# V in four pieces, block stores by column, block loads in pairs, first modulation behind the rows

## The chip, the core and the metric

The kernel runs on one core of a Trainium2 chip. The metric is the device time of one execution in microseconds (us). A core has five engines, each with its own instruction queue: TensorE (PE, matmuls), VectorE (DVE), ScalarE (ACT), GpSimd (POOL) and SyncE (SP), which here issues nearly all transfers. The transfers themselves run on 16 DMA engines, which all queues share. Engines wait for each other by semaphores alone.

## What is computed

`x` has 8 batches of 512 rows of 512 values. Two layers are applied, each with a residual:

```python
x = x + L0(x, mask, cond, ...)      # attention
x = x + L1(x, cond, ...)            # quaternion rotation
# L0
q, k, v = (x @ Wq.T, x @ Wk.T, x @ Wv.T)        # 16 heads of 32
scores = einsum('bhsd,bhtd->bhst', q, k) * 32 ** -0.5
attn = softmax(where(mask, -inf, scores))
out = einsum('bhst,bhtd->bhsd', attn, v) @ Wo.T
xn = out / sqrt(mean(out * out) + 1e-6) * rms_scale
shift, sc = split(silu(cond) @ Wc.T + bc)
return xn * (1 + sc) + shift
# L1: a product with a fixed 512 x 512 rotation made of cond, q_right and gate
```

## The kernel before

The first third (`projections`) computes q, k and v of all batches and writes them to scratch memory in HBM. The rest (`attention`) goes through 32 units, a unit being 4 heads of one batch (NG = 4 units in a batch). The order of the work is written out by hand: GROUPS lists the groups of tiles, v counts them. Groups 0 to 29 are whole units of 16 tiles (4 heads i by 4 chunks c of 128 rows), and the last two units are split into four half groups. Each engine runs through the same list of tiles with its own offsets: PE computes scores 7 tiles ahead, DVE adds the mask and finds the row minimum, ACT takes the exponential, then a tile of probabilities must be transposed before it can be multiplied by V.

Three of the four heads of a unit are transposed on PE (L831) and copied out of PSUM by ACT (L1074) or DVE (L965). The first head (i = 0) goes another way. DVE transposes its four tiles in blocks of 32 x 32 (`block`, L956) into `blocks`, with partitions (a, p), a = 0 to 3, p = 0 to 31, and free dimensions (k, j, c, t). What is left, to exchange blocks a and k, is done by two transfers through the scratch `blocks_scratch`, of 1 MB each way: four stores (L749), one for each a, from 32 partitions, and four loads (L755), one for each a, into `turned_probs`. Each load waits for its own store (`blocks_out[a]`, L754). DVE may overwrite `blocks` for the next group when all four stores have landed (L951). PE multiplies a group by V (`values`, L866) two tiles into the next group; its first head waits for the loads (`moved`).

SP's queue is in order. For each group v it does, in this order: the result store of an earlier chunk and the load of an x chunk (both wait for GpSimd); `move_blocks(v)`, the stores and loads above; `load_unit(u + 2)`, eight loads of 256 KB with the rows of q and k for the unit after the next; at the first group of a batch the modulation (`load_mod`, 512 KB, one row of 4 KB to all partitions); and at the second group of a batch the whole V of the next batch (`load_v`, 1 MB). In group 4 (v == NG) V of batch 1 and the modulation of batch 0 are loaded first, ahead of the group's block stores. GpSimd needs the modulation in `shift` (L1177), the last thing in its list for group 4; in its list for group 5 stand `rms` (L1183) and `spread_inverse` (L1155), whose result PE transposes in `turn_scale` (L840).

Two buffers each of V and the modulation alternate by batch. The semaphore `v_in[b % 2]` tells PE that V of batch b is there.

Of the kernel before, what the change touches and what calls it, by code (L numbers as in the profile page):

```python
# [14 lines left out]
B, S, E = 8, 512, 512  # L15
H, D = 16, 32
C = 128
KC = E // P
TC = S // P
HG = P // D  # L20
NG = H // HG
# [3 lines left out]
RING, SLOTS = 10, HG + 1  # L25
# [59 lines left out]
def f32(ap):  # L85

    return ap.bitcast(F32)
# [514 lines left out]
def attention(nc, held, block, banks, x, scr, rows, scores, late, late_x, kept, done, mod_scr, out, rot, ident, wo_hi,  # L602
# [5 lines left out]
    with ExitStack() as ctx:  # L608
        def sb(name, shape, dt=F32):
            return ctx.enter_context(nc.sbuf_tensor(name, shape, dt))  # L610

        def sem(name):
            return held.enter_context(nc.semaphore(name))
# [7 lines left out]
        v_sb = f32(values_and_k[:, :, :, :])  # L621
        turned_probs = sb("turned_probs", [P, SLOTS, TC, S])
        blocks = sb("blocks", [P, TC, TC, TC, D])
# [20 lines left out]
        v_in = kept.v_in  # L644
# [3 lines left out]
        out_act, out_dve = sem("out_act"), sem("out_dve")  # L648
        scale_turned, scale_out = sem("scale_turned"), sem("scale_out")
        valued, normed = sem("valued"), sem("normed")  # L650
        blocks_out = [sem(f"blocks_out{a}") for a in range(TC)]
        moved = sem("moved")
        o_hi_ready, o_ready = sem("o_hi_ready"), sem("o_ready")
        y_ready = sem("y_ready")
        squared = sem("squared")
# [22 lines left out]
        def outs(eng, n):  # L678

            return BY_ACT[:n + 1].count("1" if eng == "act" else "0")  # L680
# [16 lines left out]
        def span(chunks):  # L697

            return slice(chunks[0] * P, (chunks[-1] + 1) * P)
# [34 lines left out]
        @block.sync  # L734
        def _(sp):
            def load_unit(u):
                if u >= 2:
                    sp.wait_ge(scored, TILES * (u - 1))
                for r in range(4):
                    rows.load_q(sp, u, r)  # L740
                    if u < U - 1:
                        rows.load_k(sp, u, r)

            def move_blocks(v):
                sp.wait_ge(blocked, TC * (v + 1))
                if v >= 2:
                    sp.wait_ge(moved, 16 * TC * (v - 1))
                for a in (0, 2, 1, 3):
                    sp.dma_start(scr["blocks"][v % 2, a].rearrange("(k p) t -> p k t", p=D),  # L749
                                 blocks[a * D:(a + 1) * D].rearrange("p k j c t -> p k (j c t)")).then_inc(blocks_out[a], 16)  # L750
                if v >= 2:
                    sp.wait_ge(valued, v - 1)
                for a in (0, 2, 1, 3):
                    sp.wait_ge(blocks_out[a], 16 * (v + 1))  # L754
                    sp.dma_start(turned_probs[:, HG * v % SLOTS, a, :], scr["blocks"][v % 2, a]).then_inc(moved, 16)  # L755

            def load_v(b):
                if b >= 2:
                    sp.wait_ge(valued, NG * (b - 1))
                if b == B - 1:  # L760
                    sp.wait_ge(held_stored, 16 * TC)
                sp.dma_start(v_sb[:, b % 2], scr["v"][b].rearrange("c p e -> p c e")).then_inc(v_in[b % 2], 16)

            def load_mod(b):
                if b >= 2:
                    sp.wait_ge(summed, TC * (b - 1))
                sp.dma_start(mod[:, b % 2], mod_scr[b].partition_broadcast(P)).then_inc(mod_in[b % 2], 16)

            def load_x(b, c):
                if TC * b + c >= 2:  # L770
                    sp.wait_ge(rotated, TC * b + c - 1)
                sp.dma_start(x_s[:, c % 2], x[b, c * P:(c + 1) * P, :]).then_inc(x_in[c % 2], 16)

            def store(m):
                b, c = m // TC, m % TC
                sp.wait_ge(rotated, m + 1)
                sp.dma_start(out[b, c * P:(c + 1) * P, :], acc[:, c % 2]).then_inc(stored[c % 2], 16)

            def store_held(c):
                sp.wait_ge(held_copied, c + 1)  # L780
                sp.dma_start(scr["v"][B - 1, c], held_v).then_inc(held_stored, 16)

            for j in range(4):
                sp.wait_ge(qk_stored[j], 16 * 4 * B)
            sp.wait_ge(mod_stored, 16)
            for v, (u, chunks) in enumerate(GROUPS):
                b, g = u // NG, u % NG
                if v == NG:
                    sp.wait_ge(held_made, TC)
                    load_v(1)  # L790
                    load_mod(0)
                if 1 <= v <= NG:
                    store_held(v - 1)
                if NG <= v < NG + LATE_X:
                    load_x(v // NG - 1, v % NG)
                if v >= NG + 2:
                    store(v - NG - 2)
                if chunks == ALL:
                    move_blocks(v)
                if u + 2 < U:  # L800
                    load_unit(u + 2)
                if v == V - 6:
                    sp.wait_ge(valued, NG * (B - 1))
                    for r in range(4):
                        rows.load_k(sp, U - 1, r)
                if g == 0 and b > 0:
                    load_mod(b)
                if g == 1 and 0 < b < B - 1:
                    load_v(b + 1)
                if v == V - 5:  # L810
                    for c in range(TC):
                        sp.dma_start(late_x[:, c], x[B - 1, c * P:(c + 1) * P, :]).then_inc(late_in[c], 16)
            store(CHUNKS - 1)
            for j, m in enumerate(LATE):
                sp.wait_ge(late_rotated, j + 1)
                sp.dma_start(out[m // TC, m % TC * P:(m % TC + 1) * P, :], late_out[j]).then_inc(late_stored[j], 16)
            for j in range(2):
                sp.wait_ge(stored[j], 16 * len(range(j, CHUNKS, 2)))
            for j in range(3):
                sp.wait_ge(late_stored[j], 16)  # L820

        @block.tensor
        def _(pe):
# [20 lines left out]
            def values(v, part):  # L844

                u, chunks = GROUPS[v]
                b, g, cols = u // NG, u % NG, span(chunks)
                if part == 0 and v % NG == 0:
                    pe.wait_ge(v_in[b % 2], 16 * (b // 2 + 1))
                if part == 0:  # L850
                    if v == 0:
                        pe.wait_ge(qk_lo_ready, 2 * NG * B)
                    pe.wait_ge(out_act, outs("act", FIRST[v + 1] - 1))
                    pe.wait_ge(out_dve, outs("dve", FIRST[v + 1] - 1))
                    if v > 0:
                        pe.wait_ge(normed if v <= POOL_GROUPS else o_ready, v)
                for i in range(HG):
                    h = HG * g + i
                    to, of = value_ps[i * D:(i + 1) * D, cols], turned_probs[:, (HG * u + i) % SLOTS, part, cols]
                    if i == 0 and chunks == ALL:  # L860
                        if part == 0:
                            pe.wait_ge(moved, 16 * TC * (v + 1))
                        to = to.rearrange("p (c a t) -> p a c t", c=TC, a=TC)
                        of = turned_probs[:, HG * u % SLOTS, :, part * P:(part + 1) * P].rearrange(
                            "p a (c t) -> p a c t", c=TC)
                    last = pe.matmul(to, v_sb[:, b % 2, part, h * D:(h + 1) * D], of,  # L866
                                     start=(part == 0), stop=(part == TC - 1))
                if part == TC - 1:
                    last.then_inc(valued, 1)
# [35 lines left out]
            for n, (v, u, i, c) in enumerate(ORDER):  # L905
                t = n - FIRST[v]
# [19 lines left out]
            for part in range(TC):  # L926
                values(V - 1, part)
# [13 lines left out]
        def _(dve):  # L941
# [7 lines left out]
            def block(n):  # L949
                v, u, i, c = ORDER[n]  # L950
                dve.wait_ge(exped, n + 1)  # L951
                if n == 0:
                    dve.wait_ge(projected, (TC + 2 * NG) * (B - 1) + 2 * NG)
                for a in range(TC) if c == 0 and v > 0 else ():
                    dve.wait_ge(blocks_out[a], 16 * v)
                dve.transpose(blocks[:, :, :, c, :].rearrange("p k j t -> p j k t"),  # L956
                              probs[:, n % RING, :].rearrange("p (j k t) -> p j k t", j=TC, k=TC)).then_inc(blocked, 1)

# [68 lines left out]
            for n, (v, u, i, c) in enumerate(ORDER):  # L1027
                t = n - FIRST[v]
# [282 lines left out]
```

## Time and profile before

| | us |
|---|---|
| median of 3 runs (lowest to highest) | 828.29 (827.21 to 829.35) |
| the profiled execution | 826.24 |
| its span, from the first to the last instruction | 824.4 |
| PE busy, share of the span | 799.9, 97% |
| ACT busy | 605.8, 73% |
| DVE busy | 606.6, 74% |
| GpSimd busy | 517.5, 63% |
| DMA: moved, mean rate | 216.63 MB, 263 GB/s |

The attention part begins at about 260 us, where the page's slices of DVE and ACT fill up. Busy time of PE is modelled and includes overlapping instructions. A number in brackets behind a row of the timeline is the idle time of the engine ahead of it, and what ended it.

### The profile page before, as it was taken

What the parts mean: (1) busy time and instruction counts of PE and PEld (TensorE: products, weight loads), DVE (VectorE), ACT (ScalarE), POOL (GpSimd) and SP (SyncE); (2) the same over time, 40 slices, a digit from 0 to 9 for tenths busy, and PEclk for the clock granted to TensorE, in tenths of its full rate; (3) what the DMA queues carried; (4) which work ended last, traced back from release to release, by engine and by line L of the source; (5) the groups of instructions that cost most, each with busy time, mean ns of one, the idle gap of its engine ahead of it and who ended that gap; (6) DMA issues with size and microseconds to landing.
All of it is one profiled execution on the core that took longest, in us unless ns stands there. A gap on an engine that the chain in (4) does not pass through costs nothing.

```text
span 824.4 us, 16423 instructions
## 1 busy us (share of the span) xinstructions
PE 799.9 (97%) x4864; PEld 597.2 (72%) x4864; DVE 606.6 (74%) x1495; ACT 605.8 (73%) x1504; POOL 517.5 (63%) x375
## 2 busy tenths in 40 slices
PE   9999999999998999999999999998999999999887
PEld 6788888888887776677677767775677677767664
DVE  4612313213227899999999999999899999997666
ACT  6222222323326899999999999999999999998772
POOL 0899992000000111288888887888788888888984
PEclk9999999999999899999999999999999999999999
DMA  8964555546388888999998999898989998998001
GB/s 286 339 222 179 204 188 207 191 155 227 128 307 290 288 279 287 331 336 322 324 319 307 305 322 334 291 307 293 321 304 336 328 313 295 327 319 294 27 27 52
DMA packets 116912, 216.63 MB, mean 263 GB/s; under 512 B 12360, under 2 KB 13000, under 8 KB 116832
## 3 DMA queue, kind: packets, MB, share of 16 engines
q1 hardware_dynamic: 116688, 215.42, 76.4%
q8 instruction: 36, 0.59, 0.3%
q14 instruction: 44, 0.36, 0.1%
q10 hardware_dynamic: 144, 0.26, 0.1%
HBM read 133.81 MB, written 81.82 MB: 262 GB/s over the span
## 4 chain that ended last, share of the span: by engine, by line
ACT 21%; PE 16%; POOL 10%; issue 8%; DMA 7%; DVE 3%; SPq 3%; DVEq 0%; ACTq 0%; POOLq 0%
ACT probs L156 15%; PE banks L831 5%; DMA blocks_scratch<-blocks 5%; ACT turned_probs L1074 5%; PE banks L866 4%; POOL late L711 4%; PE banks L137 4%; DMA turned_probs<-blocks_scratch 3%; POOL late L1212 2%; SPq L749 1%; PE banks L900 1%; PE banks L880 1%; ACT o_T L1106 1%; DVE blocks L956 1%; ACT inv_T L1090 1%
## 5 line engine op out<-in xcount | busy, mean ns | idle before, releaser
L156 ACT ACTIVATE probs<-probs,least 128x512 f32<-128x512 f32 x512 | 376.3, 775 | 3.1 <-DVE least L148 3.1
L148 DVE CUSTOM_DVE_ANT_0 probs<-banks,mask_bias 128x512 f32<-128x512 f32 x512 | 327.7, 681 | 11.3 <-PE banks L137 9.9
L831 PE MATMUL banks<-ident,probs 128*128 128x128 f32 x1568 | 232.0, 274 | 0.0
L831 PEld LDWEIGHTS banks<-ident,probs 128*128 128x128 f32 x1568 | 191.9, 141 | 43.2 <-issue 6.7
L137 PE MATMUL banks<-k_rows,q_rows 128*128 128x512 f32 x496 | 201.4, 456 | 5.8 <-DVE least L148 5.8
L1074 ACT ACTIVATE turned_probs<-banks 128x512 f32<-128x512 f32 x256 | 159.6, 643 | 16.9 <-PE banks L831 11.9
L419 DVE SCALAR_TENSOR_TENSOR late<-banks,late 128x512 fp32r<-128x512 f32 x64 | 44.0, 690 | 160.0 <-ACT late L356 160.0
L156 ACT ACTIVATION_READ_ACCUMULATOR probs<-probs,least 128x1 f32 x512 | 129.8, 254 | 0.0
L711 POOL TENSOR_TENSOR late<-rot,late 128x2048 f32<-128x2048 f32 x28 | 128.9, 4604 | 0.0
L356 ACT ACTIVATE late<-banks 128x512 fp32r<-128x512 f32 x64 | 38.2, 598 | 119.3 <-PE banks L492 113.7
L866 PE MATMUL banks<-turned_probs,v_sb 128*32 128x512 f32 (+1 forms) x1088 | 116.9, 570 | 9.1 <-DMA turned_probs<-blocks_scratch 7.6
L137 PEld LDWEIGHTS banks<-k_rows,q_rows 128*128 128x128 f32 x496 | 90.7, 190 | 35.8 <-issue 24.3
L965 DVE COPY turned_probs<-banks 128x512 f32<-128x512 f32 x136 | 93.3, 686 | 1.8 <-PE banks L831 1.6
L866 PEld LDWEIGHTS banks<-turned_probs,v_sb 128*32 128x32 f32 x1088 | 34.1, 109 | 72.2 <-issue 59.9
L1217 POOL MEMSET minus_half<- 128x1 f32 x1 | 0.1, 98 | 132.8 <-PE banks L831 132.8
L956 DVE STREAM_TRANSPOSE blocks<-probs 128x512 f32<-128x512 f32 x120 | 75.0, 680 | 0.0
L1212 POOL TENSOR_TENSOR late<-late 128x1024 f32<-128x1024 f32 x29 | 69.4, 2393 | 2.2
L349 ACT ACTIVATE v_out<-banks 128x512 f32<-128x512 f32 x28 | 16.7, 598 | 56.3 <-PE banks L492 53.0
L1164 POOL CAST o_hi<-o_T 128x512 fp32r<-128x512 f32 x29 | 17.8, 613 | 63.8 <-DVE o_T L977 56.5
L900 PE MATMUL banks<-wo_hi,o_hi 128*128 128x512 f32 x128 | 50.8, 397 | 2.4 <-DVE late L1002 2.4
L900 PE MATMUL banks<-wo_lo,o_hi 128*128 128x512 f32 x128 | 52.8, 413 | 0.0
L900 PE MATMUL banks<-wo_hi,o_lo 128*128 128x512 f32 x128 | 50.5, 395 | 0.0
(136 smaller groups left out, 1331.9 us busy)
## 6 DMA issues: line engine op xcount, KB each, us to landing
q_rows<-q_scratch SPq DMA_DIRECT2D x128, 256.0 KB, 4.7
k_rows<-k_scratch SPq DMA_DIRECT2D x124, 256.0 KB, 4.9
blocks_scratch<-blocks SPq DMA_DIRECT2D x120, 256.0 KB, 5.2
turned_probs<-blocks_scratch SPq DMA_DIRECT2D x120, 256.0 KB, 3.4
q_scratch<-late SPq DMA_DIRECT2D x64, 256.0 KB, 2.3
k_scratch<-late SPq DMA_DIRECT2D x64, 256.0 KB, 2.3
v_sb<-v_scratch SPq DMA_DIRECT2D x8, 1024.0 KB, 7.8
out<-late SPq DMA_DIRECT2D x29, 256.0 KB, 5.7
```

Of the source, the lines that this page charges most:

```text
L137: pe.matmul(self.ps[:, n % SCORE_BANKS, :], self.rows.q[:, u % 2, i, c * P:(c + 1) * P], self.rows.k_of(u)[:, i, :], start=True, stop=True ...
L148: dve.tensor_tensor_reduce(self.probs[:, n % RING, :], self.ps[:, n % SCORE_BANKS, :], self.mask_bias[:, c, :], 1.0, 3e38, ALU.add, ALU.mi ...
L156: act.activation(self.probs[:, n % RING, :], self.probs[:, n % RING, :], ACT.Exp, bias=self.least[:, n % 32:n % 32 + 1], scale=-1.0, accum ...
L419: dve.scalar_tensor_tensor(qk_lo[m % 4], proj[:, m % 4, :], QSCALE if m < NG else 1.0, late[:, m % 4, :], ALU.mult, ALU.subtract).then_inc ...
L711: return eng.tensor_tensor(to.rearrange("p j (i d) -> p j i d", i=4), rot[:, :, :, :], chunk.rearrange("p (j d) -> p j d", j=4).unsqueeze( ...
L831: last = pe.transpose(turn_bank("tile", n)[:, j * P:(j + 1) * P], probs[:, n % RING, j * P:(j + 1) * P], ident[:, :])
L866: last = pe.matmul(to, v_sb[:, b % 2, part, h * D:(h + 1) * D], of, start=(part == 0), stop=(part == TC - 1))
L900: last = pe.matmul(y_of(m), left[:, b % 2, k, t], right[:, k, :], start=(part == 0), stop=(part == 11))
L956: dve.transpose(blocks[:, :, :, c, :].rearrange("p k j t -> p j k t"), probs[:, n % RING, :].rearrange("p (j k t) -> p j k t", j=TC, k=TC) ...
L965: dve.tensor_copy(turned_probs[:, h % SLOTS, :, c * P:(c + 1) * P], turn_bank("tile", n).rearrange("p (j t) -> p j t", j=TC)).then_inc(out ...
L1074: act.activation(turned_probs[:, h % SLOTS, :, c * P:(c + 1) * P], turn_bank("tile", n).rearrange("p (j t) -> p j t", j=TC), ACT.Copy).the ...
L1212: pool.tensor_tensor(mix[:, 0:2, :], mix[:, 0:2, :], mix[:, 2:4, :], ALU.add).then_inc(paired, 1)
```

## The change

Stores: the four transfers of a group now go by k, the second of the free dimensions of `blocks`, each from all 128 partitions (a, p); on the scratch side one writes for each a the 32 rows of block column k. `blocks_out` counts by k. Loads: two transfers, each for two values of a, issued when all four stores have landed; `moved` becomes two semaphores, by parity of the group. V: `load_v` takes the chunks to load. Batch 1 is still loaded at once in group 4; V of a later batch comes in four pieces, behind the row loads of the second, third and fourth group of the batch before, and ahead of the block stores of its own first group. The first modulation is loaded in group 4 behind the row loads.

```diff
--- before.py
+++ after.py
@@ -648,8 +648,8 @@
         out_act, out_dve = sem("out_act"), sem("out_dve")
         scale_turned, scale_out = sem("scale_turned"), sem("scale_out")
         valued, normed = sem("valued"), sem("normed")
-        blocks_out = [sem(f"blocks_out{a}") for a in range(TC)]
-        moved = sem("moved")
+        blocks_out = [sem(f"blocks_out{k}") for k in range(TC)]
+        moved = [sem(f"moved{i}") for i in range(2)]
         o_hi_ready, o_ready = sem("o_hi_ready"), sem("o_ready")
         y_ready = sem("y_ready")
         squared = sem("squared")
@@ -744,22 +744,25 @@
             def move_blocks(v):
                 sp.wait_ge(blocked, TC * (v + 1))
                 if v >= 2:
-                    sp.wait_ge(moved, 16 * TC * (v - 1))
-                for a in (0, 2, 1, 3):
-                    sp.dma_start(scr["blocks"][v % 2, a].rearrange("(k p) t -> p k t", p=D),
-                                 blocks[a * D:(a + 1) * D].rearrange("p k j c t -> p k (j c t)")).then_inc(blocks_out[a], 16)
+                    sp.wait_ge(moved[v % 2], 32 * (v // 2))
+                to = scr["blocks"][v % 2].rearrange("a (k p) t -> a p k t", p=D)
+                for k in range(TC):
+                    sp.dma_start(to[:, :, k], blocks[:, k].rearrange("p j c t -> p (j c t)")).then_inc(blocks_out[k], 16)
                 if v >= 2:
                     sp.wait_ge(valued, v - 1)
-                for a in (0, 2, 1, 3):
-                    sp.wait_ge(blocks_out[a], 16 * (v + 1))
-                    sp.dma_start(turned_probs[:, HG * v % SLOTS, a, :], scr["blocks"][v % 2, a]).then_inc(moved, 16)
-
-            def load_v(b):
+                for k in range(TC):
+                    sp.wait_ge(blocks_out[k], 16 * (v + 1))
+                for a in range(0, TC, 2):
+                    sp.dma_start(turned_probs[:, HG * v % SLOTS, a:a + 2, :],
+                                 scr["blocks"][v % 2, a:a + 2].rearrange("a p t -> p a t")).then_inc(moved[v % 2], 16)
+
+            def load_v(b, chunks):
                 if b >= 2:
                     sp.wait_ge(valued, NG * (b - 1))
                 if b == B - 1:
                     sp.wait_ge(held_stored, 16 * TC)
-                sp.dma_start(v_sb[:, b % 2], scr["v"][b].rearrange("c p e -> p c e")).then_inc(v_in[b % 2], 16)
+                sp.dma_start(v_sb[:, b % 2, chunks], scr["v"][b, chunks].rearrange("c p e -> p c e")).then_inc(
+                    v_in[b % 2], 16)
 
             def load_mod(b):
                 if b >= 2:
@@ -787,14 +790,15 @@
                 b, g = u // NG, u % NG
                 if v == NG:
                     sp.wait_ge(held_made, TC)
-                    load_v(1)
-                    load_mod(0)
+                    load_v(1, slice(0, TC))
                 if 1 <= v <= NG:
                     store_held(v - 1)
                 if NG <= v < NG + LATE_X:
                     load_x(v // NG - 1, v % NG)
                 if v >= NG + 2:
                     store(v - NG - 2)
+                if g == 0 and b >= 2:
+                    load_v(b, slice(TC - 1, TC))
                 if chunks == ALL:
                     move_blocks(v)
                 if u + 2 < U:
@@ -803,10 +807,12 @@
                     sp.wait_ge(valued, NG * (B - 1))
                     for r in range(4):
                         rows.load_k(sp, U - 1, r)
+                if v == NG:
+                    load_mod(0)
                 if g == 0 and b > 0:
                     load_mod(b)
-                if g == 1 and 0 < b < B - 1:
-                    load_v(b + 1)
+                if g > 0 and 0 < b < B - 1:
+                    load_v(b + 1, slice(g - 1, g))
                 if v == V - 5:
                     for c in range(TC):
                         sp.dma_start(late_x[:, c], x[B - 1, c * P:(c + 1) * P, :]).then_inc(late_in[c], 16)
@@ -846,7 +852,7 @@
                 u, chunks = GROUPS[v]
                 b, g, cols = u // NG, u % NG, span(chunks)
                 if part == 0 and v % NG == 0:
-                    pe.wait_ge(v_in[b % 2], 16 * (b // 2 + 1))
+                    pe.wait_ge(v_in[b % 2], 16 + 64 * (b // 2))
                 if part == 0:
                     if v == 0:
                         pe.wait_ge(qk_lo_ready, 2 * NG * B)
@@ -859,7 +865,7 @@
                     to, of = value_ps[i * D:(i + 1) * D, cols], turned_probs[:, (HG * u + i) % SLOTS, part, cols]
                     if i == 0 and chunks == ALL:
                         if part == 0:
-                            pe.wait_ge(moved, 16 * TC * (v + 1))
+                            pe.wait_ge(moved[v % 2], 32 * (v // 2 + 1))
                         to = to.rearrange("p (c a t) -> p a c t", c=TC, a=TC)
                         of = turned_probs[:, HG * u % SLOTS, :, part * P:(part + 1) * P].rearrange(
                             "p a (c t) -> p a c t", c=TC)
@@ -951,8 +957,8 @@
                 dve.wait_ge(exped, n + 1)
                 if n == 0:
                     dve.wait_ge(projected, (TC + 2 * NG) * (B - 1) + 2 * NG)
-                for a in range(TC) if c == 0 and v > 0 else ():
-                    dve.wait_ge(blocks_out[a], 16 * v)
+                for k in range(TC) if c == 0 and v > 0 else ():
+                    dve.wait_ge(blocks_out[k], 16 * v)
                 dve.transpose(blocks[:, :, :, c, :].rearrange("p k j t -> p j k t"),
                               probs[:, n % RING, :].rearrange("p (j k t) -> p j k t", j=TC, k=TC)).then_inc(blocked, 1)
```

## Rows read from the trace of the kernel before

**Rows 1.** The page: span, PE's busy time, DMA share by slice (tenths).

```profile
span 824.4 us, 16423 instructions
...
PE 799.9 (97%) x4864; PEld 597.2 (72%) x4864; DVE 606.6 (74%) x1495; ACT 605.8 (73%) x1504; POOL 517.5 (63%) x375
...
DMA  8964555546388888999998999898989998998001
```

**Rows 2.** Waits: engine, line, releaser, us in total, times, longest.

```profile
PE banks L866 <- DMA turned_probs<-blocks_scratch: 7.6, 6, 2.9
...
SPq L754 <- DMA blocks_scratch<-blocks: 64.9, 26, 5.3
```

**Rows 3.** Timeline of PE, four value groups: start, us, instruction, idle before.

```profile
458.21 2.35 PE L866 MATMUL banks<-turned_probs,v_sb 128*32 128x512 f32 x20
...
507.61 3.64 PE L866 MATMUL banks<-turned_probs,v_sb 128*32 128x512 f32 x32 [0.94 <-DMA turned_probs<-blocks_scratch]
...
575.03 3.64 PE L866 MATMUL banks<-turned_probs,v_sb 128*32 128x512 f32 x32 [2.92 <-DMA turned_probs<-blocks_scratch]
...
754.25 3.64 PE L866 MATMUL banks<-turned_probs,v_sb 128*32 128x512 f32 x32 [1.10 <-DMA turned_probs<-blocks_scratch]
```

**Rows 4.** Timeline of SP's queue: a plain group, then one after V.

```profile
445.60 2.58 SPq L749 DMA_DIRECT2D blocks_scratch<-blocks  x4
450.49 3.16 SPq L755 DMA_DIRECT2D turned_probs<-blocks_scratch  x4
...
494.40 2.07 SPq L749 DMA_DIRECT2D blocks_scratch<-blocks  x4
501.57 2.14 SPq L755 DMA_DIRECT2D turned_probs<-blocks_scratch  x4
```

**Rows 5.** The page's DMA issues: count, KB each, median us from issue to landing.

```profile
blocks_scratch<-blocks SPq DMA_DIRECT2D x120, 256.0 KB, 5.2
turned_probs<-blocks_scratch SPq DMA_DIRECT2D x120, 256.0 KB, 3.4
...
out<-late SPq DMA_DIRECT2D x29, 256.0 KB, 5.7
...
mod_b<-mod_scratch SPq DMA_DIRECT2D x8, 512.0 KB, 7.0
```

**Rows 6.** DMA of 229.9:230.35 (the modulation's store ends), then 798.3:801.5 (one store).

```profile
DMA packets 9, 0.00 MB, mean 9 GB/s; under 512 B 8, under 2 KB 8, under 8 KB 9
...
DMA packets 144, 0.26 MB, mean 82 GB/s; under 512 B 16, under 2 KB 16, under 8 KB 144
...
out<-late SPq DMA_DIRECT2D x1, 256.0 KB, 2.0
```

**Rows 7.** Stretches: length, busy us of each engine, clock, DMA share, GB/s.

```profile
279.13:344.88 65.75, 64.37 (x449) 45.81 (x449) 65.19 (x179) 65.35 (x171) 12.22 (x16) 1.00 0.90 294
344.88:754.25 409.37, 402.76 (x2798) 287.96 (x2799) 398.25 (x1069) 404.91 (x1074) 346.73 (x246) 1.00 0.94 316
```

**Rows 8.** DMA of 344.88:754.25, then of 20:33 with its rates by slice.

```profile
DMA packets 69534, 129.52 MB, mean 316 GB/s; under 512 B 7462, under 2 KB 7462, under 8 KB 69479
...
GB/s 397 378 233 334 271 372 397 391 391 391 384 410 366 365 384 372 384 391 397 410 403 403 410 403 403 403 403 403 410 410 416 403 410 391 403 416 397 410 410 410
DMA packets 2572, 5.05 MB, mean 388 GB/s; under 512 B 166, under 2 KB 166, under 8 KB 2571
```

**Rows 9.** Timeline of SP and PE: first group's stores, loads and values.

```profile
266.49 2.63 SPq L749 DMA_DIRECT2D blocks_scratch<-blocks  x4
271.85 2.25 SPq L755 DMA_DIRECT2D turned_probs<-blocks_scratch  x4
...
279.13 3.64 PE L866 MATMUL banks<-turned_probs,v_sb 128*32 128x512 f32 x32
```

**Rows 10.** Timeline of GpSimd and PE: inverses of group 4.

```profile
343.80 0.61 POOL L1155 COPY inv_d<-inv 128x512 f32<-128x512 f32 x1
...
349.22 0.60 PE L840 MATMUL banks<-ident,inv_d 128*128 128x128 f32 x4
```

## The prediction

> **What bounds the kernel now.** I read the page's busy shares and slices first [rows 1], then the waits of TensorE and of SP's queue [rows 2], then the value matmuls one group at a time [rows 3] and SP's queue around two groups [rows 4]. The reader should see two things. The attention part is filled on every side: in the 409.37 us from the values of group 4 to those of group 29, PE, ACT and DVE are busy 402.76, 404.91 and 398.25 us, and the DMA engines 0.94 of the time at 316 GB/s [rows 7]. That is 25 groups of 16.4 us. And the one thing from outside the compute engines that stops PE is the load of the transposed block: 7.6 us in 6 waits [rows 2], 2.92 us the longest; a group without it starts its values with no wait [rows 3]. Five of the six follow the 1 MB V load or, at the first, V and mod together; the last (1.10 us) follows the loads of K. In the group after a V load the first block comes back 7.2 us after the first store was issued (494.40 to 501.57), in a plain group 4.9 us (445.60 to 450.49) [rows 4]. So the margin is thin in both directions: little to win, about 7 us, and everything that makes stores or loads longer by more than a microsecond or two is paid in every group.
>
> **The edits, one by one.**
>
> *V in four pieces, mod behind the rows.* The bytes stay. Three more issues a batch on SP, about 0.5 us each as the block transfers are (2.14 us for four [rows 4]), against two fewer issues in each group: nothing on the path. The gain is bounded by the waits behind V: 7.6 less the 1.10 of the K loads, 6.5 us [rows 2, 3]. The price is the first modulation: its load goes from before the stores of group 4 to after that group's eight row loads. GpSimd's first shift waits for it, and queued behind that shift stand the first rms and the spread of group 4's inverses, which ran at 343.80 and which PE transposed at 349.22 [rows 10]. The load takes 7.0 us [rows 5], so one wait of 0 to 6 us appears there, once; I take 5 where nothing else is late and nothing where PE is late by more anyway.
>
> *Two loads for four.* A load used to be issued as its own store landed; now both wait until all four have landed. The data are the same 1 MB. Between the first and the last of four issues lay 2.14 and 3.16 us [rows 4], and the last took 3.4 us to land [rows 5], which in the plain group gives 453.65 + 3.4 = 457.1 against values at 458.21 [rows 3]: 1.1 us of cover. Bounds: from 1 us gained (fewer transfers) to 1 us lost in each group.
>
> *Stores by column.* This decides. Before, a store had 32 partitions outermost on both sides. Now the SBUF side has 128 partitions, but the scratch side is written as (a, p, t): 4 outermost, then 32 rows, then 2 KB, and those two cannot be merged, since column k takes 32 rows out of each block of 128. What does a small outermost count do? The trace has one transfer that can be seen alone: the store of the modulation from 8 partitions. Its end holds 8 packets under 512 B (the ninth is a row of data), where one store of 128 partitions ends with 16 among its 144 [rows 6]; those small ones are the completions of the engines that took part. So 8 outermost rows ran on 8 of the 16 DMA engines. No row shows 4 against 128. The two ends are 16 engines, where the store costs what it did, and 4, where each engine carries a quarter of every store. I take 4, since the 8-row transfer is the nearest row.
>
> The Trainium skill has a rule for the case that no row shows ("DMA: Bandwidth & Descriptors", section "Why a DMA increments its semaphore by 16 and not by 1"): a transfer uses the largest number of engines up to 16 that divides the outermost counts of both sides, and on SP's queue they are the lowest-numbered. The trace agrees at 8; by that rule all four stores of a group share the same four engines and the time is the forecast below, and by 16 engines it is one of the rivals at 820 to 835.
>
> Now the price on four engines. The stage moves 129.52 MB in 25 groups [rows 8], 5.18 MB each. Four block stores of 0.26 MB [rows 6] are 1.05 MB of it. Each of the four engines then carries 1.05/4 = 0.262 MB of stores and (5.18 - 1.05)/16 = 0.258 MB of the rest, 0.520 MB, where it carried 0.324 MB. Its rate: 316 GB/s at a share of 0.94 is 21.0 GB/s for a busy engine [rows 7]; in the fullest early stretch 388 GB/s are 24.3 GB/s [rows 8]. The stores meet little else, so 0.262 at 24.3 gives 10.8 us; the rest at the middle of the two rates, 22.6, gives 11.4 us. These follow one another: SP issues the stores, waits for all of them, then issues the loads, then rows, V, x and out, and the next stores stand behind those. Between the last store and the first load the four engines are empty: a store alone takes 2.0 us from issue to landing for about 0.7 us of data [rows 6], so about 1.3 us of start and end, with the issue 1.5 us. **One group: 10.8 + 11.4 + 1.5 = 23.7 us** in place of 16.4. PE, ACT and DVE keep their 16 us and wait for the rest; DVE's next transposes wait for the stores to land, but then take their turn while SP is still issuing rows, so they add nothing. That wait stands in DVE's queue ahead of the masks, and hence of PE's scores: it ends before PE's own wait for the load does.
>
> **Sum.** 25 groups of 23.7 us are 592.5 in place of 409.4: +183. The four groups before (65.75 us at 294 GB/s [rows 7], 4.83 MB each) have 0.236 MB of the rest, 10.4 us, so 22.7 each: +25. The first group, 266.49 to 279.13 [rows 9], had its first store back after 5.4 us and now has it after some 12, less the cover before 279.13: +4. The late mod and V pieces lie inside these waits: 0. The half groups at the end move no blocks: 0. Together +212 on the profiled execution's 826.24, 1038; the median of the runs, 828.29, lies 2 above that execution, so **1040 us**. Low end: 25.6 GB/s, the 410 GB/s of the best slices in the early stretch, and half the gap: 21.0 and 20.2 us, +131, 959. High end: 21.0 GB/s throughout and a gap of 1.8: 26.6 and 25.5 us, with 6 at the start +298, 1126.
>
> **Rivals.** *Faster:* the stores spread over all 16 engines. Then the V pieces take the five waits away and the mod load lands while PE has other work: 826.2 - 6.5, about 820 us. For it: the five waits do follow V. Against: the scratch pattern, and [rows 6]. It decides if the stores show 16 completions each, and the block is back before 7 us have gone.
> The Trainium skill speaks for this rival ("SBUF — State Buffer", section "Door 1: The DMA port swizzle"): 32 adjacent partitions reach half of SBUF's DMA ports, 128 reach all. By that rule the old stores are held at half rate and the new ones come back sooner, 820 us; the trace doesn't bear it out, since the 32-partition stores land in 5.2 us beside 5.7 us for the 128-partition out stores [rows 5].
>
> *A little slower:* 16 engines, or four different ones for each store, but the loads start only after the last store, and mod is late. Half of the 1 us lost in some 20 groups is +10, mod +5, V -6.5: 835 us. For it: the cover of 1.1 us; against, again, the small outermost count.
>
> *No change:* 16 engines, and the gains and the late starts cancel: 826 to 829 us.
>
> **Chances.** Four shared engines, the forecast: 0.86. Faster at 820: 0.04. Slower at 835: 0.07. No change: 0.03. A measurement of this kernel tells about 0.3% from no change. So faster 0.04, same 0.03, slower 0.93. The forecast's bounds, 959 to 1126, hold most of its 0.86, about 0.8 in all, so they are the range.
>
> **What would show it.** Right: groups of 21 to 27 us from one value matmul to the next; PE's wait for the block about 7 us in each of some 29 groups; the first wait of SP for a store over 10 us; landings of the block stores at 10 us and more; a DMA share in the stage of about two thirds or less, because twelve engines idle while four are full; completion packets of 4 a store, some 1,440 fewer in the whole run. Wrong: stores that land in 5 us, or a share that stays above 0.9. If stores are slow but groups stay under 20 us, the step that adds the rest of the traffic behind the stores is the false one; if groups are near 27 us, the rate.

## The result, and the profile after

The changed kernel takes 1058.92 us (median of 4 runs, 1057.90 to 1061.42), 1.279 times the kernel before (827.75 us beside it; interval 1.275 to 1.283). It is slower, and by nearly what was forecast (1040 us). First the page of after: busy times, DMA share by slice, and the counts of DMA packets; the last row is the count on the page of before.

```profile
span 1057.3 us, 16416 instructions
...
PE 858.1 (81%) x4864; PEld 610.9 (58%) x4864; DVE 610.5 (58%) x1495; ACT 610.6 (58%) x1504; POOL 517.3 (49%) x375
...
DMA  9755554558555655556666555655666665556401
...
DMA packets 114800, 216.62 MB, mean 205 GB/s; under 512 B 10248, under 2 KB 10888, under 8 KB 114720
...
DMA packets 116912, 216.63 MB, mean 263 GB/s; under 512 B 12360, under 2 KB 13000, under 8 KB 116832
```

The bytes are the same and DVE, ACT and GpSimd are busy as long as before (PE's busy time is longer; the last section says why); what fell is the DMA share in the attention part, from nines to fives and sixes [rows 1]. Fewer small packets are left, 10248 of 12360. If each of 120 stores ends with 4 completions in place of 16 (-1440), 60 loads are gone (-960) and 18 pieces of V have come (+288), 10248 should remain, and 10248 there are. So the counts fit four engines for every store by column.

The stretches of after that answer to [rows 7]: the four groups before group 4 and the 25 groups behind it (length, busy us of each engine, clock, DMA share, GB/s).

```profile
287.32:381.88 94.56, 71.89 (x448) 47.71 (x449) 63.72 (x171) 64.28 (x166) 9.50 (x11) 0.86 0.57 203
381.88:986.78 604.90, 450.48 (x2798) 298.42 (x2799) 400.51 (x1069) 408.93 (x1070) 351.95 (x254) 0.86 0.60 215
```

The span grew by 232.9 us: 195.5 in the 25 groups (604.90 against 409.37), 28.8 in the four before (94.56 against 65.75), 8.2 in the start of the first values (287.32 against 279.13), 0.4 at the end. A group takes 24.2 us. PE's waits for the block, and one group on SP's queue and on PE:

```profile
PE banks L872 <- DMA turned_probs<-blocks_scratch: 180.8, 30, 10.4
```

```profile
457.49 5.02 SPq L750 DMA_DIRECT2D blocks_scratch<-blocks  x4
473.44 0.90 SPq L756 DMA_DIRECT2D turned_probs<-blocks_scratch  x2
...
481.51 0.58 SPq L750 DMA_DIRECT2D blocks_scratch<-blocks  x1
```

```profile
454.18 5.23 PE L872 MATMUL banks<-turned_probs,v_sb 128*32 128x512 f32 x32 [5.99 <-DMA turned_probs<-blocks_scratch]
```

PE waited for the block in 6 groups before [rows 2], and now waits in all 30, 180.8 us in all. From the first store to the first load there are 15.95 us (457.49 to 473.44), where [rows 4] have 4.9 to 7.2.

Which engines the stores share can be read from the DMA share of that group, in three stretches (their bounds were read off in steps of 0.4 us):

```profile
462.20:472.60 10.40, 9.71 (x63) 7.97 (x62) 10.22 (x32) 10.40 (x28) 9.63 (x5) 1.00 0.26 101
472.60:475.00 2.40, 0.00 (x0) 0.00 (x0) 2.20 (x7) 2.40 (x7) 2.23 (x4) 0.89 0.12 21
475.00:486.40 11.40, 7.81 (x51) 3.88 (x52) 3.81 (x9) 3.65 (x11) 2.09 (x3) 0.72 1.02 358
```

In the first stretch the four stores are issued (the last at 462.51) and little else is left, and about a quarter of the 16 engines is busy, at 101 GB/s, 25 for each of four. So the four stores of a group share the same four engines; had each had four of its own, all 16 would have been busy. In the second the engines are nearly empty, until the first load's data move; in the third the rest of the traffic fills all 16.

### The profile page after: what moved, and what is told of

Same layout as the page of the kernel before. It is cut to its first block, busy times and chain, and to the rows that moved or that the text cites. A ratio compares the mean times of both kernels' runs of the same rounds, so it can differ in the third digit from the quotient of the medians.

```text
span 1057.3 us, 16416 instructions
## 1 busy us (share of the span) xinstructions
PE 858.1 (81%) x4864; PEld 610.9 (58%) x4864; DVE 610.5 (58%) x1495; ACT 610.6 (58%) x1504; POOL 517.3 (49%) x375
## 2 busy tenths in 40 slices
DMA packets 114800, 216.62 MB, mean 205 GB/s; under 512 B 10248, under 2 KB 10888, under 8 KB 114720
## 4 chain that ended last, share of the span: by engine, by line
DMA 35%; PE 32%; SPq 22%; issue 6%; POOL 4%; DVE 1%; ACT 0%; DVEq 0%; POOLq 0%; ACTq 0%
DMA blocks_scratch<-blocks 32%; PE banks L490 8%; PE banks L492 8%; PE banks L491 8%; SPq L107 6%; SPq L103 6%; SPq L750 5%; PE banks L872 2%; PE banks L837 2%; SPq L756 2%; PE banks L137 2%; DMA turned_probs<-blocks_scratch 2%; POOL late L711 1%; SPq L764 1%; PE banks L906 1%
## 5 line engine op out<-in xcount | busy, mean ns | idle before, releaser
L156 ACT ACTIVATE probs<-probs,least 128x512 f32<-128x512 f32 x512 | 364.0, 723 | 2.2 <-DVE least L148 2.2
L872 PE MATMUL banks<-turned_probs,v_sb 128*32 128x512 f32 (+1 forms) x1088 | 171.3, 789 | 181.9 <-DMA turned_probs<-blocks_scratch 180.8
L1080 ACT ACTIVATE turned_probs<-banks 128x512 f32<-128x512 f32 x256 | 149.3, 596 | 230.1 <-PE banks L872 216.9
L872 PEld LDWEIGHTS banks<-turned_probs,v_sb 128*32 128x32 f32 x1088 | 45.7, 145 | 287.9 <-issue 282.9
L156 ACT ACTIVATION_READ_ACCUMULATOR probs<-probs,least 128x1 f32 x512 | 102.7, 201 | 0.0
L1183 POOL TENSOR_TENSOR late<-late,mod_b 128x512 f32<-128x512 f32 x28 | 35.7, 1275 | 35.2 <-DMA mod_b<-mod_scratch 24.0
```

Of the source, the lines that this page charges most:

```text
L156: act.activation(self.probs[:, n % RING, :], self.probs[:, n % RING, :], ACT.Exp, bias=self.least[:, n % 32:n % 32 + 1], scale=-1.0, accum ...
L1080: act.activation(turned_probs[:, h % SLOTS, :, c * P:(c + 1) * P], turn_bank("tile", n).rearrange("p (j t) -> p j t", j=TC), ACT.Copy).the ...
```

## The experiments

Three questions were open: whether the stores alone make the time, whether it is the count of engines or the pattern of the rows, and what the other edits do by themselves.

**Undo the stores alone.** The changed kernel, stores per block a from 32 partitions as before.

```diff
-    for k in range(TC): sp.dma_start(to[:, :, k], blocks[:, k] ...)
+    for a in (0, 2, 1, 3): sp.dma_start(scr["blocks"][v % 2, a] ..., blocks[a * D:(a + 1) * D] ...)
```

> The changed kernel with its four stores put back to one per block a, from 32 partitions each; V in pieces, the late modulation and the two loads stay. My theory (four shared DMA engines carry every store by column): the stores run on 16 engines again and groups fall from 24.2 to 16.2 to 17 us; 815 to 840 us. Rival (the loads that wait for all four stores, the pieces of V or the late modulation make the time): stays above 1000 us. Completion packets: the 120 stores end with 16 each again, so under 512 B 10248 + 1440 = 11688.

Measured: 848.79 us, 1.024 times before (1.017 to 1.031); under 512 B 11688 packets, as worked out. 210 of the 231 us go with the stores. The remaining 21 us lie above the range expected, so the other edits cost something too: PE waits for the block 17 times, and once, 5.7 us, for the inverses.

```profile
PE banks L872 <- DMA turned_probs<-blocks_scratch: 21.3, 17, 4.5
```

**The stores alone.** The kernel before, stores by column, four loads that wait for all stores, since each now needs all of them.

```diff
-    for a in (0, 2, 1, 3): sp.dma_start(scr["blocks"][v % 2, a] ..., blocks[a * D:(a + 1) * D] ...)
+    for k in range(TC): sp.dma_start(to[:, :, k], blocks[:, k] ...)
+    for k in range(TC): sp.wait_ge(blocks_out[k], 16 * (v + 1))
```

> The kernel before with the stores by column alone; still four loads, but each waits for all four stores, since each now needs all of them; V whole and the first modulation early as before. My theory: nearly the whole loss, 1045 to 1075 us, groups of about 24 us. Rival (the other edits): 815 to 850 us. The whole 1 MB of V ahead of the stores may make the groups after it some us longer than others, but the four engines carry the same bytes.

Measured: 1077.93 us, 1.302 times (1.293 to 1.312), a little above the range and 19 us slower than the whole change. Its PE waits 201.7 us for the block, in 30 waits. The stores alone explain the loss. Beside them the other edits give 19 us back, while they lose 21 us without them. The trace shows two places for it. SP needs some 1.75 us to issue the four loads of a group, where two take some 0.9 in after; and a group that starts right behind a whole V is longer (511.75 to 537.82, 26.1 us; the next one 23.4 us). No run separates the two.

```profile
529.61 1.76 SPq L756 DMA_DIRECT2D turned_probs<-blocks_scratch  x4
```

**Two engines.** The changed kernel, each store cut into two of 64 partitions: 2 outermost on the scratch side, the same rows to the same places.

```diff
-    sp.dma_start(to[:, :, k], blocks[:, k] ...)
+    for a in (0, 2):
+        sp.dma_start(to[a:a + 2, :, k], blocks[a * D:(a + 2) * D, k] ...)
```

> The changed kernel with each store by column cut into two of 64 partitions, so that the scratch side is 2 outermost in place of 4; the same rows of 2 KB to the same places, 8 transfers a group in place of 4. My theory, by the same sum: two shared engines carry 1.05/2 = 0.52 MB of stores at 24.3 GB/s, 21.6 us, + 11.4 + 1.5 = 34.5 us a group, 10.8 us more than on four engines in some 29 groups: about 1370 us (1300 to 1450), and 2 completion packets a store. Rival (the scattered rows in scratch, or reading all 128 partitions, make a store slow, whatever the count of engines): the same rows, so near 1059 us, up to 1100 for four more issues.

Measured: 1353.97 us (one run), inside the range. The 25 groups from the values of group 4 to those of group 29, then 12 us in which little but stores is left:

```profile
427.37:1281.64 854.27, 457.64 (x2798) 299.73 (x2799) 402.10 (x1069) 408.90 (x1070) 351.81 (x254) 0.75 0.43 152
...
510.00:522.00 12.00, 4.53 (x28) 3.45 (x27) 5.92 (x19) 8.55 (x24) 8.07 (x7) 0.80 0.13 51
```

A group takes 34.2 us (854.27 / 25) against 34.5 worked out. While the stores run alone the DMA share is 0.13 at 51 GB/s: two engines of 16, at 25 GB/s each, as in after. There are again 10248 packets under 512 B, 2 for each of 240 half stores. The rows and the bytes are those of after, and the half transfers are even smaller, so neither the scattered rows nor the reading of many partitions makes the time; the outermost count does. From four engines to two a group grew by 10.0 us (34.2 against 24.2), where the sum has 10.8.

**All partitions on 16 engines.** The scratch is laid out by column, so that a store has 128 outermost on both sides. The loads go by k into 32 partitions, each behind its own store.

```diff
-    to = scr["blocks"][v % 2].rearrange("a (k p) t -> a p k t", p=D)
-    sp.dma_start(to[:, :, k], blocks[:, k] ...)
+    sp.dma_start(scr["blocks"][v % 2, k], blocks[:, k] ...)
...
-    for a in range(0, TC, 2):
-        sp.dma_start(turned_probs[:, HG * v % SLOTS, a:a + 2, :], ...)
+    for k in range(TC):
+        sp.wait_ge(blocks_out[k], 16 * (v + 1))
+        sp.dma_start(turned_probs[k * D:(k + 1) * D, HG * v % SLOTS], scr["blocks"][v % 2, k].rearrange("(a p) t -> p a t", p=D))
```

> The changed kernel with the scratch laid out by column: a store by column goes from all 128 partitions to 128 rows of 2 KB in a row, so that 128 is outermost on both sides; the loads then go by k into 32 partitions each, and each waits for its own store alone. V in pieces and the late modulation stay. My theory: 16 engines, groups of 16.1 to 16.6 us, 812 to 835 us, 16 completions a store. Rival (reading a column from all 128 partitions is what is slow): above 900 us.

Measured: 830.30 us, 1.002 times (0.999 to 1.005): the same as before, inside the range. Stores land in 4.1 us (5.2 before [rows 5], 4.7 with V in pieces alone), and PE waits for the block 3 times in place of 6. What keeps it from being faster is one place, on PE's timeline:

```profile
346.27 3.64 PE L871 MATMUL banks<-turned_probs,v_sb 128*32 128x512 f32 x32
356.75 1.11 PE L845 MATMUL banks<-ident,inv_d 128*128 128x128 f32 x4 [5.97 <-POOL inv_d L1160]
371.11 1.48 PE L871 MATMUL banks<-turned_probs,v_sb 128*32 128x512 f32 x9
```

From 346.27 to 371.11 there are 24.8 us where a group takes 16.2: PE stands for the inverses of group 4, and those stand on GpSimd behind the shift that waits for the late modulation.

**The other edits, one by one, and a better pair.** Each was made alone in the kernel before (V in pieces with the `load_v` lines of the change); the last row of the table is the run with the scratch by column, its modulation back ahead of the stores.

```diff
# mod alone
-    if v == NG: load_v(1); load_mod(0)
+    if v == NG: load_v(1)          # and load_mod(0) behind load_unit
# pairs alone
-    for a in (0, 2, 1, 3): wait blocks_out[a]; load block a
+    for a in (0, 2, 1, 3): wait blocks_out[a]
+    for a in (0, 2): load blocks a, a + 1
# pairs, each behind its own two stores
+    for a in (0, 1): wait blocks_out[a], blocks_out[a + 2]; load blocks a, a + 2
```

> The kernel before with the first modulation alone moved behind the row loads of group 4. My theory: PE's transposes of the inverses of group 4 wait for GpSimd, which waits for the modulation; the scratch-by-column run shows 8.7 us there (371.11 - 346.27 against 16.1). Here the stores of group 4 are also freed of 0.5 MB, worth at most the 1.4 us that its values waited. So +4 to +9 us, 832 to 837. Rival (hidden, and group 4 gains): 826 to 828 us.

> The kernel before with the two loads alone, which wait for all four stores (from 32 partitions, as before). My theory: the loads come back up to 1 to 2 us later, where the cover is about 1 us; small waits in more than the six groups, 834 to 846 us. Rival (fewer transfers gain as much): 825 to 830 us.

> The kernel before with V alone in four pieces. My theory of the waits behind V: four of the six waits (0.4, 0.9, 2.9, 0.9 us) go and the first stays, 820 to 825 us. Rival (the pieces only spread the same delay over more groups): 826 to 830 us.

> The scratch-by-column run with the first modulation put back ahead of the stores of group 4; V in pieces. My theory: the 8.7 us of that run's group 5 go, about 1.4 us in group 4 come back: 819 to 825 us, faster than the kernel before by 0.4 to 1%. Rival (the wait there has another cause): 828 to 832 us.

> The kernel before with two loads in place of four, each waiting for its own two stores alone (blocks 0 and 2, then 1 and 3, in the order of the stores), beside the run with two loads that wait for all four (847 us). My theory (the wait for all four is what costs): most of those 20 us go, 826 to 836 us. Rival (a load of 512 KB is itself slower to land than two of 256 KB): stays at 840 to 850 us.

| run | us | ratio (interval) |
|---|---|---|
| mod alone | 833.47 | 1.008 (1.005 to 1.011) |
| pairs alone, behind all four stores | 847.23 | 1.024 (1.019 to 1.029) |
| pairs, behind their own two | 840.26 | 1.012 (1.004 to 1.019) |
| V in pieces alone | 825.21 | 0.998 (0.994 to 1.001) |
| scratch by column, V in pieces | 822.29 | 0.994 (0.991 to 0.997) |

The late modulation costs 6 us, V in pieces gains 2 to 3, which the interval can't tell from nothing. The pairs cost 20 us, 1 us more than the range expected. Waiting for their own two stores they still cost 12 (3 to 16 by the interval): above my range and at the low end of the rival's. So the wait for all four has a part, some 8 us (each run against the kernel before beside it); what is left belongs to the larger load, which lands in 4.4 to 4.5 us where one of 256 KB takes 3.4 [rows 5], and to the wait for the second of its stores, and no run separates those two. In both runs PE waits 20 us or more for the block, in 9 and 10 places. V in pieces came out between my range and the rival's; the other two runs lie inside mine.

The last run is the one that beats the kernel before, by 0.3 to 0.9%. In its stage DMA is busy 0.99 of the time and a group takes 16.2 us (405.69 / 25), what PE, ACT and DVE need:

```profile
345.54:751.23 405.69, 403.00 (x2798) 287.70 (x2799) 398.48 (x1069) 404.86 (x1076) 347.28 (x246) 1.00 0.99 319
```

## Why the prediction was right

- *Stores on four engines.* Right, and shown four ways: by the count of completion packets, by the DMA share while the stores run alone (0.26), by the run that undoes the stores, and by the run on two engines. The signs named for it came: groups of 24.2 us, a DMA share of 0.60, and in each of 30 groups a wait for the block, of 6.0 us on average.
- *The price of a group.* 23.7 us worked out, 24.2 measured. In the three stretches above the stores take 10.4 us (10.8 in the sum) and the rest 11.4 (11.4); between the last store and the data of the first load lie 2.4 us where the sum has 1.5. So the gap is the term that was too small; the two groups behind that one divide nearly alike.
- *The sum.* Short by 21 us of 233: +195.5 for +183 in the 25 groups, +28.8 for +25 in the first four, +8.2 for +4 at the start, 0.4 at the end.
- *The other edits at nothing.* Not so, and here luck helped: the stores alone take 250 us more than the kernel before, where the sum gave the whole change 212. The 19 us that the other edits give back beside them brought the measured time nearer to 1040.
- *The start.* The prediction had the first store back some 12 us behind its issue; the first load was issued 14.5 us behind the first store (267.60), which is 2.5 us of the missing 4. The stores themselves were issued 1.1 us later than before [rows 9].

```profile
282.15 0.90 SPq L756 DMA_DIRECT2D turned_probs<-blocks_scratch  x2
```

- *DVE's wait for the stores costs nothing.* Right: its transposes begin at 473.50, 0.06 us behind the first load's issue, and are done long before SP's next stores at 481.51.

```profile
473.50 2.49 DVE L962 STREAM_TRANSPOSE blocks<-probs 128x512 f32<-128x512 f32 x4 [0.20 <-DMA blocks_scratch<-blocks]
```

- *The late modulation, hidden where PE is late anyway.* The wait came, 4.46 us at the inverses of group 4, and the next wait for the block was 0.80 us in place of about 6. Without the stores it costs the 6 us of the run that makes it alone; I had taken 5.

```profile
392.74 1.12 PE L846 MATMUL banks<-ident,inv_d 128*128 128x128 f32 x4 [4.46 <-POOL inv_d L1161]
...
406.90 3.64 PE L872 MATMUL banks<-turned_probs,v_sb 128*32 128x512 f32 x32 [0.80 <-DMA turned_probs<-blocks_scratch]
```

- *The loads in pairs.* The bound of 1 us lost in each group, some 30 us, holds the 20 us measured in the kernel before, but they fall in 9 places and not in every group, and the 10 us of the rival is half of them. The cover of 1.1 us was read from one plain group with median landings of a 256 KB load; the 512 KB load lands 1 us later, and that was not in it.
- *V in pieces.* Bounded by 6.5 us; alone 2 to 3. Behind the other V loads 0.2 us of waiting is left, but the first of the waits stays, since V of batch 1 is still loaded at once.
- *The rival by SBUF's ports.* The runs with V in pieces that differ in the scratch layout alone show what stores from all partitions bring on 16 engines: they land in 4.3 us where those from 32 take 4.7, their loads into 32 partitions in 4.2 where loads into all take 3.4, and the kernel takes 822.29 us (820.49 to 826.08) where it took 825.21 (822.55 to 829.16). That is a small gain, far from stores at double rate.

## What to carry to other kernels

Before the layout of a transfer is changed, look at the outermost count of both of its sides as they stand: here a count of 4 put the transfer on four of 16 engines, and where the DMA share was 0.94 those four became the bound of the whole stage. Two readings tell it without an experiment: the count of small packets says how many engines the transfers used, and the DMA share while they run alone says whether they share them. To gain the little that all partitions gave here (822.29 against 825.21 us), lay out the scratch so that the store stays contiguous across partitions, and let the load take the split.

## What was not expected

Behind many of its waits for the block, PE runs the value matmuls at the lower of its two clock levels, 1.2 GHz. In the group above the granted clock is 0.51 while they run, behind 5.99 us of waiting, and back at 1.00 from 457.49 on:

```profile
454.18:457.50 3.32, 3.32 (x17) 0.89 (x21) 0.00 (x0) 0.00 (x0) 0.00 (x0) 0.51 1.03 375
```

The 32 matmuls take 5.23 us there and 3.64 us in [rows 3]; PE's busy time on the page rose with it, to 858.1 us from 799.9. In the changed kernel the next wait is longer than that, so it should cost nothing there, though no run shows it. In the pairs alone it adds to the loss: behind a wait of 2.99 us the same matmuls take 5.34 us.

```profile
651.05 5.34 PE L868 MATMUL banks<-turned_probs,v_sb 128*32 128x512 f32 x32 [2.99 <-DMA turned_probs<-blocks_scratch]
```

The length of the wait alone does not tell when: behind 2.92 us the kernel before kept 3.64 us [rows 3], and behind 2.05 us the run with V in pieces alone took 5.34, at a granted clock of 0.68.

The four store issues themselves also became longer, 5.02 us in place of 2.07 to 2.58 [rows 4]; on two engines the eight of a group take 14.87 us, as if SP's queue were held up while the few engines are full. No run tells why.
